# Decay stage of a graph network kernel: joined loops, another order of the loads, VectorE's share of the weights from step 4

## The reference

```python
# layer 0: two hops
agg = adj @ x; x = tanh(concatenate([agg, x], 1) @ W[k])
# layer 1
Ax = adj @ x; out = 1 - 0.1 * x - 0.01 * sum(x * Ax, 1)
# layer 2 ("decay")
support = input @ weight
mask = (adj != 0); rank = cumsum(mask, axis=1); deg = rank[:, -1:]
k = minimum(deg, 100); pos = rank - (deg - k)
w = mask * where(pos > 0, 0.5 ** (k - pos), 0.0)
out = w @ support + bias
# layer 3, twice: edge sums, attention, cosine pruning, down and up
edge_feat = H.T @ V; att = softmax((Q @ edge_feat.T) * scale * H, 1); ...
```

## Time and profile before

| | us |
|---|---|
| median of 3 runs | 1664.15 (1664.0 to 1665.42) |
| the profiled execution | 1663.85 |
| its span | 1662.0 |
| TensorE busy | 1466.7 (88%) |
| VectorE busy | 1171.7 (70%) |
| ScalarE busy | 755.8 (45%) |
| transfers | 578.45 MB, mean 348 GB/s |

### The profile page before, as it was taken

How to read it: one execution, slowest core, us unless ns; L and a number is a source line. 1 busy time by engine, 2 the same in 40 slices (tenths; PEclk the granted TensorE clock), 3 DMA queues, 4 the chain that set the end, 5 groups by cost and what they waited for, 6 DMA issues and landing times.

```text
span 1662.0 us, 24795 instructions
## 1 busy us (share of the span) xinstructions
PE 1466.7 (88%) x10364; PEld 630.0 (38%) x10389; DVE 1171.7 (70%) x1603; ACT 755.8 (45%) x709; POOL 349.9 (21%) x308
## 2 busy tenths in 40 slices
PE   7899999898899998677888799999997788797896
PEld 2244433333344343333332344443443333332443
DVE  3440212666413997999989798116997999989898
ACT  0000101665311775999920333014776999900443
POOL 0000000000000894444400000002993444200000
PEclk9999999999999999999899999999999988999999
DMA  9979598799799996566599999999993666699995
GB/s 401 426 298 406 237 416 362 258 376 421 313 426 382 426 421 250 206 247 245 208 375 426 425 425 424 426 425 424 416 412 139 247 246 248 243 405 425 409 426 231
DMA packets 55967, 578.45 MB, mean 348 GB/s; under 512 B 6320, under 2 KB 6576, under 8 KB 16816
## 3 DMA queue, kind: packets, MB, share of 16 engines
q1 hardware_dynamic: 55856, 576.87, 85.5%
HBM read 575.14 MB, written 1.70 MB: 347 GB/s over the span
## 4 chain that ended last, share of the span: by engine, by line
PE 56%; DMA 19%; DVE 14%; issue 7%; ACT 3%; SPq 0%; POOL 0%; DVEq 0%; POOLq 0%; ACTq 0%
PE ps L702 54%; DMA arena<-adj_t 7%; DMA slot<-adj 7%; DVE shared L1625 4%; DVE slot L1812 4%; DMA arena<-adj_half 3%; DMA shared<-adj_t 2%; PE ps L1125 2%; DVE shared L1812 2%; ACT shared L1247 1%; DVE slot L1841 1%; DVE shared L1841 1%; ACT shared L1305 1%; ACT shared L1352 1%; DVE slot L1776 0%
## 5 line engine op out<-in xcount | busy, mean ns | idle before, releaser
L1625 DVE CUSTOM_DVE_ANT_1 shared<-ps,slot 128x832 f32<-128x832 f32 x352 | 341.9, 1021 | 6.6 <-PE ps L702 5.5
L702 PE MATMUL ps<-shared 64*128 64x416 f32 (+3 forms) x1076 | 239.6, 503 | 100.6 <-DVE max L1625 83.1
L1305 ACT ACTIVATE shared<-shared,negmax 128x3327 f32<-128x3327 f32 x88 | 270.0, 3069 | 68.9 <-DVE negmax L1636 66.2
L702 PE MATMUL ps<-slot,cur 128*64 128x512 f32 (+1 forms) x1440 | 262.6, 515 | 14.7 <-DVE slot L1812 14.6
L639 POOL TENSOR_SCALAR cur<-shared,row_rz 128x768 f32<-128x768 f32 x32 | 70.6, 2207 | 854.5 <-DVE row_rz L1727 850.1
L702 PE MATMUL ps<-arena 64*128 64x416 f32 (+1 forms) x1072 | 209.0, 525 | 1.0 <-DMA arena<-adj 0.5
L1352 ACT ACTIVATE shared<-ps 128x2048 int16<-128x2048 int16 (+1 forms) x52 | 78.1, 1554 | 274.9 <-PE ps L1125 274.8
L702 PEld LDWEIGHTS ps<-shared 64*128 64x128 f32 (+2 forms) x1092 | 95.4, 175 | 217.6 <-DVE max L1625 127.4
L702 PEld LDWEIGHTS ps<-slot,cur 128*64 128x64 f32 x1440 | 96.4, 137 | 176.7 <-issue 153.1
L1321 ACT ACTIVATE arena<-shared,cut 128x3328 fp8e4<-128x3328 f32 x52 | 159.1, 3059 | 2.1 <-DVE cut L1763 1.2
L1776 DVE SCALAR_TENSOR_TENSOR slot<-arena,slot 128x2752 f32<-128x2752 int8 x48 | 145.0, 3021 | 5.5 <-ACT arena L1321 5.5
(11 more groups left out here) (222 smaller groups left out, 1650.8 us busy)
## 6 DMA issues: line engine op xcount, KB each, us to landing
slot<-adj SPq DMA_DIRECT2D x157, 1664.0 KB, 9.6
slot<-adj_t SPq DMA_DIRECT2D x60, 1664.0 KB, 13.8
arena<-adj_half SPq DMA_DIRECT2D x52, 832.0 KB, 6.7
shared<-adj SPq DMA_DIRECT2D x26, 1664.0 KB, 14.7
arena<-adj_t SPq DMA_DIRECT2D x25, 1664.0 KB, 22.7
shared<-adj_t SPq DMA_DIRECT2D x22, 1664.0 KB, 14.1
arena<-adj SPq DMA_DIRECT2D x15, 1664.0 KB, 15.3
slot<-adj SPq DMA_DIRECT2D x2, 1024.0 KB, 19.3
```

Of the source, the lines that this page charges most:

```text
L702: return pe.matmul(o, l, r, start=start, stop=stop, skip_group_check=True)
L1305: act.activation(bufs[b][:, 0:N], bufs[b][:, 0:N], ACT.Exp, bias=negmax[:, b:b + 1], accum_out=rowsum[:, b:b + 1]).then_inc(exp_done, 1)
L1625: dve.tensor_tensor_reduce(out=pieces3(bufs[k % len(bufs)], c), in0=pieces_psum(piece_place(name, k, c)[0]), in1=pieces3(slot_of(name, k), ...
```

## The change

Five edits:
- ACT_STEPS is 4 instead of 10.
- Block k = 6 of edge0 gets slot 4 (the left hats), which lies over the early weights, and waits until decay_w has been used (support_psum 3). The slots of the blocks behind it move by one.
- SP's order: 6, 5, 7 and 8 halves of decay0 and 8, 8 and 10 of decay1, and behind each group one block of edge0, seven blocks in all.
- The two loops of TensorE's counting are one over 52 steps, count(step) from 0; VectorE makes the masks of steps 26 and 27 behind steps 24 and 25. ScalarE's square_part(4, 1) and root_part(4, 1) come behind the weights of step 1 instead of step 0.
- hop0: VectorE's copy of the middle part comes between the two marks of the last block. On TensorE the last two counts are written behind the loop.

```diff
-ACT_STEPS = 10
+ACT_STEPS = 4
...
+            elif name == "edge0" and k == 6:
+                slot, free = 4, BASE["decay0"]
+                count[slot] += 1
...
+                    if name == "edge0" and home == 4:
+                        sp.wait_ge(support_psum, 3)
...
-            decay_stream(0, range(NB))
-            ahead = 6
-            for j in range(ahead):
-                decay_stream(1, range(NB)[4 * j:4 * j + 4])
+            ahead = 7
+            for j, (q, ks) in enumerate(((0, range(0, 6)), (0, range(6, 11)), (0, range(11, 18)),
+                                         (0, range(18, NB)), (1, range(0, 8)), (1, range(8, 16)), (1, range(16, NB)))):
+                decay_stream(q, ks)
                 late_stream("edge0", adj, first=j, last=j + 1)
-            decay_stream(1, range(4 * ahead, NB))
...
-                if k:
+                if 0 < k < NB - 1:
                     count_block(k - 1)
+            count_block(NB - 2)
             count_block(NB - 1)
...
+            def count(step):
+                for c in range(2):
+                    by_act, by_dve = weights_made(0, step - 1, c)
+                    if step:
+                        pe.wait_ge(relu_act, by_act)
+                        if by_dve:
+                            pe.wait_ge(relu_dve, by_dve)
+                    if step < 2 * NB:
+                        own_bits(step, c)
+                if step < 2 * NB:
+                    carried_bits(step)
+            count(0)
...
-                for c in range(2):
-                    own_bits(0, c)
-                carried_bits(0)
                 for k in range(NB):
-                    count(k)
+                    count(q * NB + k + 1)
...
-                    if q == 0 and k == 0:
+                    if q == 0 and k == 1:
                         square_part(4, 1)
                         root_part(4, 1)
...
                         if part.start == 0:
+                            early_evac(0, "hop0")
                             landed(dve, "hop0", k)
...
-            early_evac(0, "hop0")
...
-                if q:
-                    mask_of(0, q)
-                    mask_of(1, q)
...
-                    if k + 2 < NB:
-                        mask_of(k + 2, q)
+                    if q * NB + k + 2 < 2 * NB:
+                        mask_of((k + 2) % NB, q + (k + 2) // NB)
```

More of the change, by code:

```diff
@@ L888, in _, with own_bits, carried_bits @@
             support_part(2)
[L889 to L899, removed]
-                    for h in range(2):
[L901 to L912, removed]
-                    for c in range(2):
-                        by_act, by_dve = weights_made(q, k, c)
+            def own_bits(step, c):
+                q, k = divmod(step, NB)
+                if c == 0:
+                    pe.wait_ge(block_done, BASE[f"decay{q}"] + k + 1 + EARLY_RING)
+                o, w = QUART_CHUNKS[c]
+                for h in range(2):
+                    mm(bank(2 * h + c, w), tri, nbr[step % 4][:, h * QUART + o:h * QUART + o + w], stop=False)
+            def carried_bits(step):
+                q, k = divmod(step, NB)
+                row = NB - 1 - k
+                for c, (o, w) in enumerate(QUART_CHUNKS):
+                    for h in range(2):
+                        group = slice(ROWS32 * (2 * c + h), ROWS32 * (2 * c + h + 1))
+                        mm(bank(2 * h + c, w), later_blocks[group, row:row + 1].to_broadcast([ROWS32, P]),
+                           block_totals[q][group, 0:w], start=False).then_inc(tri_done, 1)
+            def count(step):
+                for c in range(2):
+                    by_act, by_dve = weights_made(0, step - 1, c)
+                    if step:
                         pe.wait_ge(relu_act, by_act)
@@ L919, in count @@
                             pe.wait_ge(relu_dve, by_dve)
[L920 to L923, removed]
+                    if step < 2 * NB:
[3 more added lines that the diff above has]
+            count(0)
+            for q in range(2):
                 def weigh(k, q=q):
@@ L1559, in mask_of @@
                 dve.wait_ge(decay_used, q * NB + k + 1)
-                dve.tensor_scalar(nbr[(2 * q + k) % 4], slot, 0.0, None, ALU.not_equal).then_inc(block_done, 1)
+                dve.tensor_scalar(nbr[(q * NB + k) % 4], slot, 0.0, None, ALU.not_equal).then_inc(block_done, 1)
             mask_of(0, 0)
```

## The result

The changed kernel takes 1654.56 us (median of 3 runs, 1654.37 to 1655.34), the kernel before 1664.15: a ratio of 0.9943 [0.9926, 0.9961], 9.6 us less. The profiled execution took 1655.34 us (span 1653.5), against 1663.85.

A forecast was written before the change was run, and what follows sets the result against it. Late half-block loads were taken to pace the decay stage's second half. Gains 0.8 + 1.9 + 5.8 + 0.6 - 0.1 = 9.0 us from 1663.85 gave 1654.9, median 1655.1; forecast 1655.0, range 1651 to 1660.

The forecast's parts named there:

- start and share (to weigh 10): Decay stage start to step 10: moved square and VectorE's share from step 4 together gain 0.8 us.
- seam: Between decay halves, steps 24 to 26: joined loops take 5.3 us instead of 7.18, gaining 1.9 us.
- second half: Decay steps 26 to 50: with fewer late loads, 67.96 us falls to 60.65 plus 1.5 lost, gaining 5.8 us.
- seven blocks, att0: Seven edge0 blocks loaded ahead let att0's loads start earlier, removing VectorE's 0.59 us load wait: gain 0.6 us.
- hop0: End of hop0: VectorE's copy moved ahead of the second mark starts TensorE's last counts 0.1 us late: -0.1 us.
- burst loss: Second half of the decay stage: four edge0 blocks among the halves, backlogs growing 0.7 us each, lose 1.5 us in all.
- rival A: Each of four edge0 blocks among the decay halves still stalls TensorE: 4.7 us lost, time 1658.4; chance 0.17.
- What I had named for 1.7 us: Decay start: if the shorter pause at step 1 kept full clock, the sum would be 1.7 us better; counted as nothing.
- The mask of step 3: Decay start: VectorE's mask comes about 1 us later, wanted only after step 1's matmuls; costed at nothing, 1 us without cover.
- B: Decay stage: queue already full at 350 GB/s, each edge0 block adds 4.05 us; slower, 1667.6 us; chance 0.06.
- C: Decay stage: queue hides all blocks and the start brings 2.5 us; gain 12.2, time 1652; chance 0.15.
- D: Late loads return elsewhere, in edge0's queue or att0, so nothing is gained: 1663 to 1664 us; chance 0.07.

The follow-up runs named there:

- e6: Kernel after with edge0's seven early blocks loaded as 14 half blocks spread over the stage: 1652.65 us, ratio 0.9923 to the kernel before.
- e12: Kernel after with edge0's early blocks halved and hop0's copy back behind both marks: 1651.94 us, ratio 0.9917 to the kernel before.
- e10: Kernel after with the join undone, the two halves counted in separate loops again: 1654.22 us, ratio 0.9932 to the kernel before.
- e1: Kernel before with only the new order of SP's loads and block 6 of edge0 in slot 4: 1657.90 us, ratio 0.9956.
- e5: Kernel after with edge0's fifth block issued behind 38 halves instead of 34, the sixth behind the last half: 1653.99 us, ratio 0.9927 to the kernel before.
- e3: Kernel before with only the counting loops joined into one run of 52 steps: 1665.25 us, ratio 1.0001.
- e4: Kernel before with only ScalarE's square and root of part 1 moved behind the weights of step 1: 1661.71 us, ratio 0.9981.
- e8: Kernel after with the share undone (ACT_STEPS = 10): 1655.66 us, ratio 0.9945 to the kernel before.
- e2: Kernel before with only ACT_STEPS = 4, VectorE's share from step 4: 1664.58 us, ratio 0.9999.
- e9: Kernel after with ScalarE's square and root of part 1 behind the weights of step 0 again: 1656.26 us, ratio 0.9947 to the kernel before.

## Why the prediction was right, and where its steps were not

The forecast was 1655.0, the time 1654.56. Step by step, gains in us:

| step | predicted | profiled pair | verdict |
|---|---|---|---|
| start and share (to weigh 10) | 0.8 | 1.82 | too small: pause and clock |
| 10 to 24 | 0 | -0.62 | burst |
| seam | 1.9 | 0.06 | not reached: burst |
| second half | 5.8 | 6.73 | part of the burst fell earlier |
| seven blocks, att0 | 0.6 | 0.57 | right |
| hop0 | -0.1 | -0.17 | right |

*The main mechanism holds.* I said that the second half loses its time to loads, and that without it the 24 steps take 60.65 us. e6, e12 and e10, without load stalls there, measured 60.57; e1 alone, 60.53. The terms are right one by one as well: in e6 steps 29, 30, 36 and 38 take 0.35, 0.60, 0.35 and 0.85 us more than 2.44, for the 0.35, 0.59, 0.35 and 0.8 of the sum.

*The burst loss is the step that I had twice wrong: in its size and in its place.* I counted 1.5 us, all in the second half, and built it on backlogs that grow by 0.7 us a group. Measured against the 100.15 us that 10 to 50 takes in e6, the loss is 103.12 - 100.15 = 3.0 us in the profiled execution and 1.4 in the next, so 1.5 is met by one of two. TensorE's waits behind the blocks issued at 325.82 and 345.99 us (0.73 and 1.78) lie in the first half and on the seam. e5 speaks against the growth. What fits better is in the prediction too, as the doubt of rival A: a block of 4.05 us against 3.9 us of slack in the ring. A half issued behind it lands after 10.5 to 11.6 us. As a rival A fell by its price, 4.7 us; its mechanism was at work at 1.4 to 3.0, where a half landed too late. The Trainium skill (DMA: Bandwidth & Descriptors, Queues, rings and completion order) says that each DMA engine takes the descriptors of a ring in order; the 11.6 us and the 9.1 us with halved blocks agree.

*The seam.* The step "5.3 us" was right for a seam with loads in time: 5.42 in e3, e6 and e12. I missed that in the kernel after the seam would be where a late half is waited for (1.78 us), and that the old seam's pause is time that the queue uses. Join alone: 1.76 gained at the seam and lost behind it (e3). Join undone: nothing lost (e10). Of the 1.9 us the change as it stands gains none that a run shows; they come with the halved blocks.

*The share.* I bounded it at 2.3 to 3.5 us for six steps, then walked the orders through and kept almost nothing. Weigh 4 to 10 takes 18.04 to 18.08 us with neither the share nor the square changed, 17.80 with the square alone (e4, e8), 17.88 or 17.89 with the share, and e2 and e8 show no change in the whole time. The walk-through was right in its result: weigh 4, 8 and 10 come 1.60, 1.20 and 1.78 us earlier than before, which is its 0.6, 0.2 and 0.8 and 1.0 us more from the start. Step 7 takes 3.51 us (3.02 without the share): VectorE's weights of step 8 start at 316.81, right behind the last of the four split instructions, and TensorE goes on at 317.60 when they are done; step 4 takes 3.43 us (3.02), and those of step 5 start at 307.23, behind an instruction of layer 1's layernorm (L1435). These two eat what the others gain.

*The start was mis-sized, at "by the rows the clock has fallen before the pause that goes, so I count nothing".* The row was right: the clock had fallen by 291.6 us, weigh 0 took 2.10. But it falls a second time, behind the pause, and a window of 14 us (0.76) hides that. Cut at 290 and 296 us, the trace of before has 0.99, 0.72 and 0.60, and the last is what weigh 1 ran at. In all 14 profiled executions weigh 1 tells the kernels apart, weigh 0 doesn't: weigh 0 is slow in 8 of 14, with the square moved or not; weigh 1 is slow (2.14 to 2.29 us) in five of the six without the move and takes 1.25 us in all eight with it. Weigh 4 starts between 305.66 and 306.16 us in the eight, between 306.44 and 309.15 in the six. Of the 2.89 us gained by weigh 2, 1.67 are the earlier start of weigh 1, and 1.22 come behind it, 0.89 of them weigh 1 itself at full clock. What I had named for 1.7 us (the Trainium skill, TensorE: Matmul & The Clock Gate, Part 1: throttled is the default state, activity releases it) agrees with the fall behind the pause and with the full clock without it, and it should have had a chance of its own. That the pause causes the second fall rests on this count and on the order of events in e9. It is not enough by itself: the sixth execution without the move, e3, has the pause and no second fall. Its granted clock is 0.72 from 290 to 296 us, as before, and 1.00 from 296 to 300:
```profile
295.58 0.60 PE L702 MATMUL ps<-shared 128*128 128x512 bf16 x2 [1.57 <-ACT shared L1250]
...
297.11 1.25 PE L702 MATMUL ps<-shared,arena 128*64 128x512 bf16 x12
```
What decides between the two stays open.

*What was given back at the start.* The mask of step 3, costed at nothing because it is wanted only after weigh 1, is waited for 1.16 us at 301.60. I had named that 1 us as the price without cover; with TensorE 2.89 us earlier the cover was gone.

*Two errors cancelled.* 1.0 us more at the start (1.82 for 0.8) stand against a second half, seam and 10 to 24 that together brought 6.17 instead of 7.7. The sum was right to 0.5 us, but each part only to 1 or 2.

*Rivals.* B needed 350 GB/s to be a capacity: the same place now runs 416, and the halved blocks 412 over 30 us. C was wrong in its bursts and half right in its start: it had 2.5 us there, the profiled pair has 1.82, and weigh 10 starts at 323.59, not before 323. e6 and e12, without the bursts and 2.25 us shorter from weigh 0 to 10, are at 1652.65 and 1651.94, which is C's 1652. The limit of about 358 GB/s a core in the Trainium skill (DMA: Bandwidth & Descriptors, Specifications) stands against 416 measured here again. D would have had the gain come back in edge0 or att0: weigh 51 to att0 is 95.31 us in both, and att0 lost its 0.59 us wait.

*A better version.* The split of the seven blocks gives 2.9 us on top (1652.65 against 1655.53 in one series). The ratios to before are 0.9923 and 0.9937 and their intervals overlap, so the whole time alone does not settle it; the stage does (10 to 50 in 100.15 us in e6 and e12, 101.5 or more in every kernel with whole blocks).

## What to carry to other kernels

When bulk loads run ahead on the queue of a shallow ring, compare the time of one bulk transfer with the slack of the ring, and not only the mean rates: if it is longer, try to cut it before moving it around. A pause that an earlier stage has may be what lets a queue catch up, so removing it pays only once the queue has slack. A granted clock averaged over more than a few microseconds should be cut at the pauses before an edit of one of them is priced at nothing.

## What the runs showed of the hardware

TensorE's clock also falls within the busy stage, behind single pauses: 2.89 us at weigh 1 in e1, e2 and e9, and in e3, where a late load holds TensorE for 2.48 us. Here is that place and the window behind it:
```profile
429.96 0.86 PE L702 MATMUL ps<-shared 128*128 128x512 bf16 x4 [2.48 <-DVE shared L1574]
...
431.08 2.29 PE L702 MATMUL ps<-shared,arena 128*64 128x512 bf16 x12
```
```profile
430.00:434.00 4.00, 4.00 (x22) 1.55 (x23) 1.72 (x2) 1.52 (x3) 0.00 (x0) 0.63 0.02 4
```
A weigh of 1.25 us took 2.29, at a mean granted clock of 0.63 (0.50, the lower of its two levels, from 432 to 434 us). e2 has the same at 433.48, behind 2.92 us. In all, e2, e3 and e4 have two such weighs each in the second half, behind waits of 2.18 to 2.92 us; the two executions of the kernel before have three waits of 2.05 to 2.46 us each, one of them that of the earlier trace rows, and all six passed at full clock. The length of the pause does not tell the two apart, and the runs do not show what does. So a late load costs its wait and sometimes up to 1.5 us more: 1.04 for the weigh and 0.43 for the counting matmuls behind it (1.44 against 1.01). While the queue sets the pace the next wait for a load takes that back, 1.4 us each in e2, e3 and e4; behind the last loads nothing does.

The queue takes a half block of 832 KB from issue to landing in 4.6 to 5.6 us where it moves 350 GB/s; at 412 to 416 GB/s it takes 7.1 to 9.1 in e6, whose transfers are all halves, and 10.5 to 11.6 right behind a whole block in the kernel after.

The part after att0 took between 1018.5 and 1024.1 us in the 14 profiled executions, with no edit in it; what varies there is open, and it is why differences of 1 to 2 us between kernels are read from the stage and not from the medians.
